# Moving the adapter products of the next two tiles, and the copies around them, in a two-adapter kernel

## The chip, the core and the metric

The kernel runs on one core of one Trainium2 chip. The metric is the device time of one execution in microseconds. Five engines work side by side: PE (TensorE, matmuls), DVE (VectorE), ACT (ScalarE), POOL (GpSimd) and SP (SyncE, which only issues transfers here). Each engine works through its own list of instructions in order, and an instruction that waits for a semaphore holds up everything behind it on its engine.

## What is computed

The input is 64 sequences of 64 rows with 1024 columns, so 4096 rows. First each sequence gets the correction of its own low-rank adapter (rank 16, picked by an index), then a dense layer with eight low-rank experts, of which the two best are weighed by a softmax. Both are added to their input.

```python
def _L0_cond_ref(x, A, B, adapter_ids):
    Bx = jnp.einsum('bni,bri->bnr', x, B[adapter_ids])
    return jnp.einsum('bnr,bor->bno', Bx, A[adapter_ids])        # SCALING is 1
def _L1_cond_ref(x, language_ids, W, Wr, A, B):
    base = jnp.einsum('btd,od->bto', x, W)
    logits = jnp.einsum('btd,ed->bte', x, Wr)                    # + 5.0 at the row's language
    topw, topi = jax.lax.top_k(logits, 2)
    gates = jnp.sum(jax.nn.one_hot(topi, E) * jax.nn.softmax(topw)[..., None], axis=-2)
    h = jnp.einsum('btd,erd->bter', x, A)
    return base + 2.0 * jnp.einsum('bter,bte,eor->bto', h, gates, B)
x = x + _L0_cond_ref(x, L0_cond_A, L0_cond_B, itok_B_4_50)
x = x + _L1_cond_ref(x, itok_B_0_7, L1_cond_W, L1_cond_Wr, L1_cond_A, L1_cond_B)
```

## The kernel before

The 4096 rows are 32 tiles of 128 rows. Every number is split into a high and a low part (`_hi`, `_lo`), and a product is made of three matmuls. The order of the work on each engine is written out by hand, and semaphores tie the engines together.

**What a tile needs.** DVE turns x (`turn_x_half`, `xT_part`), the rows of B (`bT_part`) and of A (`aT_part`). PE makes the B products (`make_bx`). ACT swaps halves of the result (`swap_part`), DVE adds them (`bx_half_part`), ACT shifts quarters (`pair_part`), and four DVE instructions (`bx_rest`) make `bx_t`. With it and the A rows PE makes the L0 products (`add_l0`), which add the first adapter into the bank that holds x. ACT and DVE split the sum into high and low parts, and PE multiplies it with the weights. The first 512 columns of that product hold the experts' rows and the router's logits. DVE chooses the experts (`choose_experts`) and weighs them (`weigh_experts`, whose last instruction makes `gated`; ACT makes one exponential, `exp_part`), PE turns `gated` (`turn_gated`), DVE copies it (`gated_t_part`, which makes `gt_hi` and `gt_lo`), and PE adds the expert products (`add_lora`, `pair_lora`; "lora products" below).

**Direct tiles.** Tiles 0 to 7 (`K = 8`) are multiplied in full, three parts each (`make_part`), in a loop over `n`. `bx_tiles(n)` says for which tiles the loop makes B products at the start of `n`: tile 2 at n=1, two tiles at n=2, 4 and 6, tile 9 at n=7. Meanwhile POOL makes sums of weight blocks (`t_chunk`, ten instructions each, four chunks, and `t_chunk_lo`, two each), which ACT rounds (`t_split`). In tile `n` DVE runs, in order: `bx_half` and `bx_rest` of the tiles in `bx_tiles(n)`, `choose_experts`, `weigh_experts`, `x1_lo_part(n+1)`, `gated_t_part(n)`, then transposes.

**Pairs.** Tiles 8 to 31 are twelve pairs `q` of tiles `a` and `b`. Each pair's other columns take seven products of block sums instead of eight. PE runs per pair: first columns of `a` (`pair_first_part(q, 0)`, 24 matmuls of 512 columns), four products of 12 matmuls each with `turn_gated(a)` among them, lora products of `a`, B products of `a+2`, first columns of `b`, L0 products of `a+2`, B products of `b+2`, two products, `turn_gated(b)`, one product, lora products of `b`, L0 products of `b+2`. In all pairs but the last the work for the next two tiles is woven in (`more`). `z_out` tells PE that ACT has copied the first columns out of their bank.

## Time and profile before

| | us |
|---|---|
| median of 3 runs (lowest, highest) | 548.58 (547.61, 553.17) |
| the profiled execution | 550.68 |
| its span, first to last instruction | 548.9 |
| mean granted TensorE clock | 0.988 |

| engine | busy us | share of the span |
|---|---|---|
| PE | 516.4 | 94% |
| DVE | 383.7 | 70% |
| POOL | 278.8 | 51% |
| ACT | 274.6 | 50% |

PE is busy nearly throughout, so the time is the sum of its products and of the short stretches in which it waits. Twelve pairs of nearly equal length follow the direct tiles, the first of them from 167.74 us. Where the page or an answer names a wait, the engine that was waited for stands behind the arrow. Such a row is read with the question what made that engine late.

### The profile page before, as it was taken

The page shows a single profiled execution, that of the slowest core. Times are in us where ns is not written, and L with a number is a line of the kernel's source. Part 1 is how long each engine was busy: PE and PEld are TensorE (multiplying, and loading weights), DVE is VectorE, ACT ScalarE, POOL GpSimd, SP SyncE. Part 2 cuts the span into 40 slices and gives each one's busy share as a digit, 9 for nine tenths or more (in the row PEclk, how much of TensorE's full clock was granted, in tenths as well). Part 3 has the DMA queues.
Part 4 walks back from the last instruction along what each step waited for, and adds up shares of the span by engine and source line. Part 5 has one row for each costly group of instructions (what it writes and reads, how often), then busy time and mean ns, then how long its engine had stood idle before and what let it go on. Part 6 is the DMA issues. An engine that isn't in the chain of part 4 may idle for free.

```text
span 548.9 us, 9809 instructions
## 1 busy us (share of the span) xinstructions
PE 516.4 (94%) x3356; PEld 462.6 (84%) x3356; DVE 383.7 (70%) x908; ACT 274.6 (50%) x617; POOL 278.8 (51%) x259
## 2 busy tenths in 40 slices
PE   7799999699989999999999999999998999999997
PEld 6688899599879878897987889898888989888896
DVE  5769666656857868586776858687685868777622
ACT  5446433333355645646464564555465554646521
POOL 5443328949975844455353545536354454535020
PEclk9699999999999999999999999999999999999999
DMA  8933523432242241524234151424316142430201
GB/s 311 325 95 100 144 77 95 125 92 87 73 125 87 83 169 39 168 70 128 97 102 149 39 189 60 133 81 111 141 53 193 43 135 78 114 136 1 79 27 51
DMA packets 31158, 60.45 MB, mean 110 GB/s; under 512 B 4348, under 2 KB 20476, under 8 KB 31108
## 3 DMA queue, kind: packets, MB, share of 16 engines
...
q8 instruction: 27, 0.44, 0.3%
...
## 4 chain that ended last, share of the span: by engine, by line
PE 63%; DVE 14%; issue 7%; ACT 6%; POOL 6%; DMA 4%; ACTq 0%; DVEq 0%; POOLq 0%
PE o_bank L730 24%; PE o_bank L739 12%; PE x_bank L739 9%; PE o_bank L706 5%; PE x_bank L612 4%; DMA a_in<-in_L_cond_A_dram,a_run 4%; ACT bx_pair L936 3%; PE b_bank L588 2%; PE o_bank L693 2%; DVE xs L1191 2%; PE x_bank L706 2%; POOL a_t L429 2%; POOL t_raw L493 2%; PE o_bank L682 2%; DVE bx_all L1342 1%
## 5 line engine op out<-in xcount | busy, mean ns | idle before, releaser
L730 PE MATMUL o_bank<-w_hi,xs 128*128 128x512 f32 x384 | 125.9, 399 | 0.1
L529 POOL TENSOR_TENSOR xs<-xt,xs 128x512 fp32r<-128x512 f32 x36 | 47.1, 1308 | 118.2 <-ACT xs L996 69.2
L693 PE MATMUL o_bank<-w_hi,xs 128*128 128x324 f32 (+1 forms) x336 | 91.8, 347 | 0.0
L730 PEld LDWEIGHTS o_bank<-w_hi,xs 128*128 128x128 f32 x384 | 72.1, 188 | 18.0 <-issue 2.2
L540 POOL TENSOR_TENSOR a_t<-a_raw,a_t 64x1024 fp32r<-64x1024 f32 x22 | 52.9, 2403 | 45.0 <-DVE bx_t L1349 44.0
L730 PE MATMUL o_bank<-w_lo,xs 128*128 128x512 f32 x192 | 75.4, 392 | 0.0
L400 POOL DMA_INDIRECT a_in<-in_L_cond_A_dram,a_run x64 | 60.8, 950 | 19.4 <-issue 19.2
L1314 DVE STREAM_TRANSPOSE a_raw<-a_in 128x1024 f32<-128x1024 f32 x32 | 64.7, 2021 | 2.8 <-DMA a_in<-in_L_cond_A_dram,a_run 2.8
L693 PEld LDWEIGHTS o_bank<-w_hi,xs 128*128 128x128 f32 x336 | 60.7, 191 | 5.5 <-issue 1.0
L1234 DVE STREAM_TRANSPOSE xt<-x_near 128x512 f32<-128x512 f32 x48 | 57.9, 1209 | 0.5 <-issue 0.5
L693 PE MATMUL o_bank<-w_lo,xs 128*128 128x324 f32 (+1 forms) x168 | 57.3, 341 | 0.0
L1191 DVE TENSOR_TENSOR xs<-x_bank,xs 128x512 fp32r<-128x512 f32 x64 | 43.2, 684 | 16.3 <-ACT xt L978 16.1
L1065 ACT ACTIVATE expd<-top 128x1 f32<-128x1 f32 x32 | 9.4, 295 | 82.6 <-DVE top L1369 82.6
L739 PE MATMUL x_bank<-t_w,xs 128*128 128x324 f32 x288 | 48.2, 315 | 0.0
L739 PE MATMUL o_bank<-w_hi,xs 128*128 128x324 f32 x192 | 47.9, 316 | 0.0
L739 PE MATMUL x_bank<-w_hi,xs 128*128 128x324 f32 x192 | 47.9, 316 | 0.0
L739 PEld LDWEIGHTS x_bank<-t_w,xs 128*128 128x128 f32 x288 | 43.6, 188 | 2.3 <-issue 2.2
L936 ACT COPY bx_pair<-bx_half 32x128 f32<-32x128 f32 x120 | 35.5, 296 | 19.0 <-DVE bx_half L1334 16.6
L730 PEld LDWEIGHTS o_bank<-w_lo,xs 128*128 128x128 f32 x192 | 36.2, 188 | 7.5
L909 ACT CAST a_t<-a_raw 128x1024 fp32r<-128x1024 f32 x32 | 33.6, 1051 | 17.1 <-DVE a_raw L1314 16.8
L406 POOL DMA_INDIRECT b_in<-in_L_cond_B_dram,b_run x32 | 30.8, 964 | 20.1 <-DVE a_t L1191 8.8
L1044 ACT COPY out_sb<-o_bank 128x376 f32<-128x376 f32 (+1 forms) x36 | 16.2, 460 | 44.9 <-PE o_bank L706 44.9
...
## 6 DMA issues: line engine op xcount, KB each, us to landing
...
a_in<-in_L_cond_A_dram,a_run POOLq DMA_INDIRECT x64, 3.5
...
```

Source lines behind the costliest of these rows:

```text
L400: pool.indirect_dma_start(a_in[:, m % 2, b, :], None, l0_A_runs, bass.IndirectOffsetOnAxis(ap=a_run[:, m * BPT + b:m * BPT + b + 1], axis= ...
L529: nc.gpsimd.tensor_tensor(xs[:, slot, 1, :, :], raw, xs[:, slot, 0, :, :].bitcast(F32), ALU.subtract).then_inc(ss_lo, 1)
L540: nc.gpsimd.tensor_tensor(lower, a_raw[Q:P, m % 2, :], lower.bitcast(F32), ALU.subtract)\
L693: mm = pe.matmul(O[part][:, 0:hi - lo], x1_at(n, c // CB, low)[:, c % CB, :], w[:, c, lo:hi], start=(k == 0), stop=(k == K3 - 1), skip_gro ...
L706: mm = pe.matmul(bank_out[:, skip:skip + hi - lo], gt[:, n % 2, :], lb[:, lo:hi], start=False, stop=(k == 2), skip_group_check=True)
L730: mm = pe.matmul(O[0][:, 0:hi - lo], xs[:, raw_slot(j, c // CB), low, c % CB, :], w[:, c, lo:hi], start=(k == 0), stop=(k == K3 - 1), skip ...
L739: mm = pe.matmul(bank_out[:, 0:H], xs[:, slot, low, c, :], w[:, c, :], start=(start and k == 0), stop=(k == 3 * CB - 1), skip_group_check= ...
L909: nc.scalar.copy(a_t[:, m % 2, :], a_raw[:, m % 2, :]).then_inc(a_hi_ready, 1)
L936: nc.scalar.copy(bx_pair[q * SQ:(q + 1) * SQ, :], bx_half[o * SQ:(o + 1) * SQ, :]).then_inc(pair_ready, 1)
L1191: return nc.vector.tensor_tensor(dst, raw, hi.bitcast(F32), ALU.subtract)
L1234: nc.vector.transpose(xt[:, m % 2, chunks(h), :].rearrange("p k (g i) -> p k g i", i=SQ), src[:, chunks(h), :, :]).then_inc(turned_s, 1)
L1314: nc.vector.transpose(raw.rearrange("p (k i f) -> p f k i", k=C, i=SQ), a_in[:, m % 2, :, :].rearrange("p b (f r) -> p f b r", r=R)).then_ ...
```

## The change

The B products of the next pair's both tiles now stand together, after 12 of the 24 matmuls of the first columns of `b` (`3 * CB` is 12). In the pairs ACT puts both halves of x into the bank ahead of the swaps, and copies x1 (`keep_raw`) ahead of `copy_cd`; DVE makes its transposes ahead of `bx_half(a+2)`, makes `aT_part(b+2)` between `bx_half(a+2)` and `bx_rest(a+2)`, and copies the turned gates of `b` ahead of `bx_rest(b+2)`. In the direct tiles `bx_rest` of the second of two tiles moves behind `weigh_experts`, and `turn_gated` waits accordingly for fewer steps. POOL's `t_chunk` run one tile earlier (m = 3 to 6 in place of 4 to 7), as does the place of ACT's `t_split` within its tile. The L0 products of tile 9 and the split of it move to the end of the direct tiles.

```diff
--- before.py
+++ after.py
@@ -514,15 +514,17 @@
                 pool.wait_ge(a_lo_ready, m + 1)
                 reload_b(m + 2)
                 reload_a(m + 2)
-                if 4 <= m < 4 + CB:
-                    if m == 4:
+                if m < 3 + CB:
+                    if m == 3:
                         pool.wait_ge(w_lo_dve, len(LO_DVE))
                         pool.wait_ge(w_lo_act, len(LO_ACT))
-                    t_chunk(m - 4)
-                    pool.wait_ge(t_step, 10 * (m - 3))
-                if m >= 6:
-                    t_chunk_lo(m - 6)
-                    pool.wait_ge(t_lo, 2 * (m - 5))
+                    t_chunk(m - 3)
+                    pool.wait_ge(t_step, 10 * (m - 2))
+                if m == 3 + CB:
+                    t_chunk_lo(0)
+                if m >= 3 + CB:
+                    t_chunk_lo(m - 2 - CB)
+                    pool.wait_ge(t_lo, 2 * (m - 1 - CB))
 
             def s_lo(q, which, slot, raw):
                 pool.wait_ge(ss_hi, 4 * q + which)
@@ -713,7 +715,7 @@
             def pair_lora(n, part, bank_out):
                 lora_products(n, part, bank_out).then_inc(so_psum, 1)
 
-            def pair_first_part(q, side):
+            def pair_first_part(q, side, bx=()):
 
                 j = 2 * q + side
                 if q == 0 and side == 0:
@@ -724,6 +726,9 @@
                 lo, hi = PARTS[0]
                 for k in range(K3):
                     c = k // 3
+                    if k == 3 * CB:
+                        for m in bx:
+                            make_bx(m)
                     if k % (3 * CB) == 0:
                         pe.wait_ge(sl_ready, HB * j + c // CB + 1)
                     low, w = ((0, w_hi), (0, w_lo), (1, w_hi))[k % 3]
@@ -821,15 +826,14 @@
                 make_part(n, 0, 0, K3).then_inc(h_psum, 1)
                 add_l0(n + 1)
                 make_part(n, 1, 0, K3)
-                turn_gated(n, bx_count(bx_made(n)))
+                turn_gated(n, bx_count(bx_made(n) - 1) + 1)
                 make_part(n, 2, 0, 12)
-                if n == K - 1:
-                    add_l0(K + 1)
                 pe.wait_ge(gt_ready, 2 * (n + 1))
                 add_lora(n, 0)
                 add_lora(n, 1)
                 make_part(n, 2, 12, K3)
                 add_lora(n, 2)
+            add_l0(K + 1)
 
             for q in range(PAIRS):
                 a, b = K + 2 * q, K + 2 * q + 1
@@ -856,12 +860,9 @@
                 pe.wait_ge(gt_ready, 2 * (a + 1))
                 pair_lora(a, 0, O[0])
                 pair_lora(a, 1, PA)
-                if more:
-                    make_bx(a + 2)
-                pair_first_part(q, 1)
+                pair_first_part(q, 1, (a + 2, b + 2) if more else ())
                 if more:
                     add_l0(a + 2)
-                    make_bx(b + 2)
                 pe.wait_ge(bc_copied, q + 1)
                 wait_sum(q, S1)
                 if q == 0:
@@ -1125,6 +1126,8 @@
                 exp_part(n)
                 if n + 1 < K:
                     x1_hi_part(n + 1)
+                if 3 <= n < 3 + CB:
+                    t_split(n - 3)
                 for m in turned(n)[1:] if n == 1 else turned(n):
                     xt_part(m)
                 if n == K - 2:
@@ -1136,17 +1139,12 @@
                 out_part(n, 1)
                 if n < K - 1:
                     a_hi_part(n + 2)
-                if n == K - 1:
-                    split_b(K + 1)
-                if 3 <= n < 3 + CB:
-                    t_split(n - 3)
                 out_part(n, 2)
 
             for q in range(PAIRS):
                 a, b = K + 2 * q, K + 2 * q + 1
                 more = b + 2 < T
-                if q > 0:
-                    split_b(b)
+                split_b(b)
                 s3_hi(q)
                 s2_hi(q)
                 if q == 0:
@@ -1166,20 +1164,19 @@
                 pair_out(a, 0, O[0], LA0, z_out)
                 pair_out(a, 1, PA, LA1, c11_out)
                 if more:
-                    swap_part(a + 2, a + 3)
-                    put_half(a + 2, 0)
+                    put_part(a + 2)
+                    swap_part(a + 2, b + 3)
                     pair_part(a + 2)
                     a_hi_part(b + 2)
-                    put_half(a + 2, 1)
                 exp_part(b)
                 if more:
                     raw_hi(a + 2, 0)
                     keep_raw(a + 2, 0)
                     swap_part(b + 2, b + 3)
                     raw_hi(a + 2, 1)
+                    keep_raw(a + 2, 1)
                 copy_cd(q)
                 if more:
-                    keep_raw(a + 2, 1)
                     pair_part(b + 2)
                     put_part(b + 2)
                 pair_out(b, 0, O[0], LB0, z_out)
@@ -1508,7 +1505,8 @@
             aT_part(2)
 
             for n in range(1, K):
-                for m in bx_tiles(n):
+                ahead = bx_tiles(n)[:1] if n % 2 == 0 else bx_tiles(n)
+                for m in ahead:
                     bx_half_part(m)
                     if n == 1:
                         xT_half(3, 0)
@@ -1516,10 +1514,12 @@
                 if n == 1:
                     a_lo_part(2)
                     xT_half(3, 1)
-                if n == K - 1:
-                    aT_part(K + 1)
+                for m in bx_tiles(n)[len(ahead):]:
+                    bx_half_part(m)
                 choose_experts(n)
                 weigh_experts(n)
+                for m in bx_tiles(n)[len(ahead):]:
+                    bx_rest(m)
                 if n + 1 < K:
                     x1_lo_part(n + 1)
                 else:
@@ -1534,33 +1534,34 @@
                     bT_part(m)
                 if n < K - 1:
                     aT_part(n + 2)
-                if n == K - 1:
-                    sums_of_pair(0)
+                if n == K - 2:
+                    aT_part(K + 1)
 
             for q in range(PAIRS):
                 a, b = K + 2 * q, K + 2 * q + 1
                 more = b + 2 < T
+                sums_of_pair(q)
                 if q == 0:
                     for c in range(CB):
                         t4_lo(c)
-                else:
-                    sums_of_pair(q)
-                if more:
+                if more and q > 0:
                     aT_part(a + 2)
                 choose_experts(a)
                 weigh_experts(a)
+                if q == 0:
+                    aT_part(a + 2)
                 if more:
                     turn_x_half(a + 2, 0)
                     bT_part(a + 2)
                 gated_t_part(a)
                 if more:
                     turn_x_half(a + 2, 1)
-                    aT_part(b + 2)
-                    bx_half_part(a + 2)
                     turn_x_half(b + 2, 0)
-                    bx_rest(a + 2)
                     turn_x_half(b + 2, 1)
                     bT_part(b + 2)
+                    bx_half_part(a + 2)
+                    aT_part(b + 2)
+                    bx_rest(a + 2)
                 choose_experts(b)
                 if more:
                     raw_lo(a + 2, 0)
@@ -1568,8 +1569,9 @@
                 if more:
                     raw_lo(a + 2, 1)
                     bx_half_part(b + 2)
+                gated_t_part(b)
+                if more:
                     bx_rest(b + 2)
-                gated_t_part(b)
                 out_b1(q)
                 out_b2(q)
```

On PE, around the first columns of tile `b` of a pair (here the first; `xt,b_raw` are B products, `bx_t,a_t` L0 products, `w_hi,xs` 128x512 the first columns), before:

```order
L706 MATMUL o_bank<-lb_hi,gt_lo 128x324
L588 MATMUL b_bank<-xt,b_raw 32x128 x8
L730 MATMUL o_bank<-w_hi,xs 128x512
...
L730 MATMUL o_bank<-w_hi,xs 128x512
L612 MATMUL x_bank<-bx_t,a_t 128x128 x8
L588 MATMUL b_bank<-xt,b_raw 32x128 x8
L739 MATMUL x_bank<-t_w,xs 128x324 x12
```

And of the change:

```order
L708 MATMUL o_bank<-lb_hi,gt_lo 128x324
L735 MATMUL o_bank<-w_hi,xs 128x512
...
L735 MATMUL o_bank<-w_hi,xs 128x512
L590 MATMUL b_bank<-xt,b_raw 32x128 x16
L735 MATMUL o_bank<-w_hi,xs 128x512
...
L735 MATMUL o_bank<-w_hi,xs 128x512
L614 MATMUL x_bank<-bx_t,a_t 128x128 x8
L744 MATMUL x_bank<-t_w,xs 128x324 x12
```

The B products no longer stand between the lora products and the first columns, nor behind the L0 products; both batches are inside the first columns, 12 matmuls ahead of the L0 products.

On DVE, the same stretch of a pair, from the copies of the turned gates of `a` to the choice of experts of `b`, before:

```order
L1191 TENSOR_TENSOR gt_lo<-b_bank,gt_hi 128x128
L1234 STREAM_TRANSPOSE xt<-x_near 128x512
L1314 STREAM_TRANSPOSE a_raw<-a_in 128x4x256
L1334 TENSOR_TENSOR bx_half<-b_bank,bx_swap 128x128
L1234 STREAM_TRANSPOSE xt<-x_near 128x512
L1342 TENSOR_TENSOR bx_all<-bx_half,bx_pair 128x128
L1344 TENSOR_TENSOR bx_own<-bx_all,own 128x128
L1346 CAST bx_hi<-bx_own 128x128
L1349 SCALAR_TENSOR_TENSOR bx_t<-bx_hi,minus_odd,bx_own 128x128
L1234 STREAM_TRANSPOSE xt<-x_near 128x512
L1306 STREAM_TRANSPOSE b_raw<-b_in 128x256
L1366 SCALAR_TENSOR_TENSOR logit<-is_lang,o_bank 128x8
```

And of the change:

```order
L1188 TENSOR_TENSOR gt_lo<-b_bank,gt_hi 128x128
L1231 STREAM_TRANSPOSE xt<-x_near 128x512 x3
L1303 STREAM_TRANSPOSE b_raw<-b_in 128x256
L1331 TENSOR_TENSOR bx_half<-b_bank,bx_swap 128x128
L1311 STREAM_TRANSPOSE a_raw<-a_in 128x4x256
L1339 TENSOR_TENSOR bx_all<-bx_half,bx_pair 128x128
L1341 TENSOR_TENSOR bx_own<-bx_all,own 128x128
L1343 CAST bx_hi<-bx_own 128x128
L1346 SCALAR_TENSOR_TENSOR bx_t<-bx_hi,minus_odd,bx_own 128x128
L1363 SCALAR_TENSOR_TENSOR logit<-is_lang,o_bank 128x8
```

All three transposes of x and the one of B stand ahead of `bx_half`, and the long transpose of A stands between `bx_half` and `bx_all`.

On DVE in the direct tiles (here n=2), from `bx_half` of the second tile on, before:

```order
L1334 TENSOR_TENSOR bx_half<-b_bank,bx_swap 128x128
L1342 TENSOR_TENSOR bx_all<-bx_half,bx_pair 128x128
L1344 TENSOR_TENSOR bx_own<-bx_all,own 128x128
L1346 CAST bx_hi<-bx_own 128x128
L1349 SCALAR_TENSOR_TENSOR bx_t<-bx_hi,minus_odd,bx_own 128x128
L1366 SCALAR_TENSOR_TENSOR logit<-is_lang,o_bank 128x8
```

And of the change:

```order
L1331 TENSOR_TENSOR bx_half<-b_bank,bx_swap 128x128
L1363 SCALAR_TENSOR_TENSOR logit<-is_lang,o_bank 128x8
...
L1390 TENSOR_TENSOR gated<-o_bank,gate 128x128
L1339 TENSOR_TENSOR bx_all<-bx_half,bx_pair 128x128
L1341 TENSOR_TENSOR bx_own<-bx_all,own 128x128
L1343 CAST bx_hi<-bx_own 128x128
L1346 SCALAR_TENSOR_TENSOR bx_t<-bx_hi,minus_odd,bx_own 128x128
L1188 TENSOR_TENSOR xs<-x_bank,xs 128x512 x2
L1396 CAST gt_hi<-b_bank 128x128
```

The four instructions of `bx_rest` leave the place ahead of the choice of experts and stand between `gated` and the copies of the turned gates.

## Rows read from the trace of the kernel before

**Rows 1.** Waits of PE over the whole span: waited for, us in total, times, longest.

```profile
PE o_bank L706 <- DVE gt_lo L1191: 10.5, 11, 1.1
PE b_bank L573 <- DVE gated L1393: 6.4, 3, 4.4
```

**Rows 2.** Timeline of PE, tiles 2, 4, 6, 7: start, us, operation, idle before.

```profile
68.22 1.00 PE L612 MATMUL x_bank<-bx_t,a_t 128*128 128x128 f32 x8
...
72.70 0.28 PE L573 MATMUL b_bank<-ident,gated 128*128 128x128 f32 x1
...
74.61 0.33 PE L706 MATMUL o_bank<-lb_hi,gt_hi 128*128 128x376 f32 x1
...
100.29 1.11 PE L612 MATMUL x_bank<-bx_t,a_t 128*128 128x128 f32 x8 [0.43 <-DVE bx_t L1349]
...
109.50 0.47 PE L573 MATMUL b_bank<-ident,gated 128*128 128x128 f32 x1 [4.44 <-DVE gated L1393]
...
112.78 0.33 PE L706 MATMUL o_bank<-lb_hi,gt_hi 128*128 128x376 f32 x1
...
143.79 0.33 PE L573 MATMUL b_bank<-ident,gated 128*128 128x128 f32 x1 [1.23 <-DVE gated L1393]
...
163.56 1.08 PE L612 MATMUL x_bank<-bx_t,a_t 128*128 128x128 f32 x8 [0.78 <-POOL a_t L429]
```

**Rows 3.** Stretches: us, busy PE, PEld, DVE, ACT, POOL, granted clock, DMA.

```profile
109.50:113.00 3.50, 3.50 (x15) 3.50 (x16) 3.46 (x6) 0.59 (x1) 1.30 (x2) 0.58 0.00 0
...
143.70:147.00 3.30, 3.21 (x21) 3.21 (x22) 3.27 (x7) 0.48 (x2) 3.06 (x5) 1.00 0.00 0
```

**Rows 4.** Timeline of POOL, tiles 2 and 3.

```profile
68.97 0.95 POOL L400 DMA_INDIRECT a_in<-in_L_cond_A_dram,a_run  x1 [0.30 <-issue]
80.13 2.39 POOL L429 TENSOR_TENSOR a_t<-a_raw,a_t 64x1024 fp32r<-64x1024 f32 x1 [10.21 <-ACT a_t L909]
```

**Rows 5.** Timeline of DVE in tile 4.

```profile
101.83 0.97 DVE L1342 TENSOR_TENSOR bx_all<-bx_half,bx_pair 128x128 f32<-128x128 f32 x1 [1.39 <-ACT bx_pair L936]
...
109.16 0.29 DVE L1393 TENSOR_TENSOR gated<-o_bank,gate 128x128 f32<-128x128 f32 x1
...
110.87 0.29 DVE L1191 TENSOR_TENSOR gt_lo<-b_bank,gt_hi 128x128 fp32r<-128x128 f32 x1
```

**Rows 6.** Timeline of PE, a pair in the middle, from its lora products of `a`.

```profile
339.68 0.34 PE L706 MATMUL o_bank<-lb_hi,gt_hi 128*128 128x376 f32 x1
...
346.99 1.00 PE L612 MATMUL x_bank<-bx_t,a_t 128*128 128x128 f32 x8
347.92 0.64 PE L588 MATMUL b_bank<-xt,b_raw 128*32 128x128 f32 x16
...
352.66 0.30 PE L573 MATMUL b_bank<-ident,gated 128*128 128x128 f32 x1 [0.29 <-DVE bx_half L1334]
...
355.75 0.44 PE L706 MATMUL o_bank<-lb_hi,gt_hi 128*128 128x376 f32 x1 [0.92 <-DVE gt_lo L1191]
...
358.55 0.45 PE L730 MATMUL o_bank<-w_hi,xs 128*128 128x512 f32 x1
```

**Rows 7.** Chain that ended last, same pair: start, us, work.

```profile
341.38 5.77 PE o_bank L730 x24
```

**Rows 8.** Timelines of ACT and of DVE, same pair.

```profile
341.44 0.55 ACT L929 COPY bx_swap<-b_bank 64x128 f32<-64x128 f32 x2 [0.17 <-PE b_bank L588]
...
331.45 2.01 DVE L1314 STREAM_TRANSPOSE a_raw<-a_in 128x1024 f32<-128x1024 f32 x1
333.31 0.16 DVE L1366 SCALAR_TENSOR_TENSOR logit<-is_lang,o_bank 128x8 f32<-128x8 f32 x1
...
342.02 0.29 DVE L1334 TENSOR_TENSOR bx_half<-b_bank,bx_swap 128x128 f32<-128x128 f32 x1 [0.27 <-ACT bx_swap L929]
...
343.86 0.29 DVE L1342 TENSOR_TENSOR bx_all<-bx_half,bx_pair 128x128 f32<-128x128 f32 x1 [0.43 <-ACT bx_pair L936]
...
344.77 0.35 DVE L1349 SCALAR_TENSOR_TENSOR bx_t<-bx_hi,minus_odd,bx_own 128x128 fp32r<-128x128 f32 x1
```

**Rows 9.** Timeline of PE, last pair, lora products of `a` and first columns of `b`.

```profile
530.42 0.34 PE L706 MATMUL o_bank<-lb_hi,gt_hi 128*128 128x376 f32 x1
...
531.67 0.50 PE L730 MATMUL o_bank<-w_hi,xs 128*128 128x512 f32 x1
```

## Prediction

> **What bounds the kernel now.** I read the waits of PE first, then its timeline through the direct tiles and through one pair in the middle, and only then the engines that it waits for. PE is busy 94% of the span, and the change leaves out none of its products, so it can only win or lose waits and the slow products that follow them. The waits that repeat are these. In the pairs PE waits 11 times, once in each pair that has a next one, for the copies of the turned gates of `b` [rows 1]: 0.92 us at 355.75, and 0.29 us at 352.66 for `bx_half` of the tile after next [rows 6]. In the direct tiles it waits three times for `gated`, 6.4 us together, of which 4.44 us in tile 4 [rows 1, 2], and 0.78 us for POOL ahead of the L0 products of tile 9 [rows 2]. A whole pair takes about 31.8 us, of which these waits are 1.2 us, so no edit of the waits can give much more than 4% of a pair.
>
> **The direct tiles.** A tile without a wait is the scale: from its L0 products to the turn of its gates 4.48 us (68.22 to 72.70), from there to its lora products 1.91 us, 6.39 us together [rows 2]. Tile 4 took 12.49 us from 100.29, and 0.43 us of waiting ahead of that, so it lost 6.5 us. Not all of this is waiting: after 4.44 us without work the granted clock was 0.58 in the stretch that follows [rows 3], near the lower level of 1.2 GHz, and the turn stood 3.28 us ahead of the lora products in place of 1.91. The cause is on DVE. `bx_rest` of tile 6 stands ahead of the choice of experts and meets `t_chunk(1)` on POOL; `bx_all` took 0.97 us there [rows 5] and 0.29 us in a pair, where POOL is quiet [rows 8].
>
> The change puts `bx_rest` of the second tile behind `gated`. So `gated` of tile 4 comes some 2.2 us after the L0 products (my estimate for twelve small instructions, 2.7 where POOL slows the last), against 4.48 needed, and this wait goes. What is late next is the copy of the turned gates: behind `gated` stand now the four instructions of `bx_rest` and the two of `x1_lo_part`. From the start of `gated` to the end of `gt_lo` without `bx_rest` were 2.0 us (109.16 to 111.16 [rows 5]). With `bx_rest` under POOL, 3.4 to 3.9 us (four of up to 0.97), PE's lora products find them after 2.2 + 2.0 + 3.7 = 7.9 us, where they come after 6.39. That is a new wait of 1.5 us in tile 4, and 1.2 in tile 6, where POOL has only four instructions of `t_chunk_lo`. In tile 2 nothing was lost, but `t_chunk(0)` now starts right behind the transfers issued at 68.97 (its ten instructions end near 79.5, ahead of POOL's next work at 80.13, so they delay nothing on POOL) [rows 4], and meets both the weighing and `bx_rest`: 2.7 + 2.0 + 3.7 - 6.39 = 2.0, of which I take 1.9. From below these new waits are zero: with `bx_rest` at the 1.3 us that it takes beside a quiet POOL (343.86 to 345.12 [rows 8]) the copies are ready after 5.5 us.
>
> Here a rule of the Trainium skill can be weighed. SBUF — State Buffer, section Who interferes with whom, says that DVE and GpSimd share a pair of ports as an exclusive lock, and that a DVE instruction with two SBUF inputs or in a two-port mode waits until the other's instruction is done. By that rule the price of 3.7 us holds wherever `bx_rest` meets POOL's products; the trace agrees in tile 4 (0.97 against 0.29). By the cheap rows the sum below would be 4.6 us lower.
>
> Then the rest of the direct tiles. The other two waits for `gated`, 6.4 - 4.4 = 2.0 us, go, because `bx_rest` or `aT_part(9)` no longer stand ahead of the choice. The 0.8 us for POOL's part of tile 9 goes, because these L0 products move behind all lora products of tile 7, 3 us later, and DVE's transpose for it comes a tile earlier. Restarts after these waits cost about 0.2 us each, 0.4 together. POOL's `t_chunk` and ACT's `t_split` one tile earlier cost nothing themselves: they run beside PE, and no copy on ACT now waits for POOL ahead of a swap. Sum: +1.9 (tile 2) - 6.5 + 1.5 (tile 4) + 1.2 (tile 6) - 2.0 - 0.8 - 0.4 = -5.1 us.
>
> **A pair.** I walk one pair with the rows' own times.
> 1. The first columns of `b` follow the lora products of `a` directly, and their bank must first be copied out. The last pair has no B products there and shows the price: 530.42 to 531.67, 1.25 us [rows 9]. So they start at 339.68 + 1.25 = 340.93 [rows 6] (six lora products alone take about 0.96, so 0.3 is a new wait that the B products covered).
> 2. The 24 products take 5.7 us [rows 7], and the two batches of B products between them about 1.2 (0.64 each, overlapping [rows 6]). PE reaches the L0 products at 347.8.
> 3. The chain to `bx_t`: 12 products, 343.8; B products, 345.05; the swap, then 0.58 to `bx_half` (341.44 to 342.02), 345.65; then DVE does `aT_part(b+2)`, which takes 1.86 us before the next instruction begins (331.45 to 333.31), 347.75. The four copies of `pair_part` lie beside it. `bx_rest` takes 1.26, so `bx_t` is there at 349.0 [rows 8]. POOL is idle then, and the port costs nothing. New wait: 1.2 us. The L0 products begin at 349.0, against 346.99: +2.0.
> 4. The turn of `b`'s gates comes without the B batch (-0.6) and without the 0.29 wait: +1.1. `bx_half(b+2)` must be ready for it: I get 353.55 against PE's arrival at 353.75, because x1 is kept ahead of `copy_cd` on ACT. That is a thin cover.
> 5. The lora products follow after 1.9 us, as in tile 2 [rows 2], in place of 3.09 (352.66 to 355.75 [rows 6]), since only the turn stands ahead of the copies: -0.1.
> 6. From there 2.80 us to the next pair (358.55), of which 0.1 is a slow restart after the wait: -0.2.
>
> The x and B transposes of `b+2` end near 342.7, a microsecond ahead of the B products at 343.8; were that cover gone, the wait would come in step 2 and not add to that of step 3 in full. POOL's part of A for `b+2` and its transfers start some 4 us later than now and still end ahead of the next pair's use by about as much. So a pair wins 0.2 us, 11 pairs 2.2. By the bounds: if `aT_part` did not count, step 3 would be bound by the pair copies and the wait 0.7 (11 pairs: -7); if step 4 or 5 each lose 0.3, a pair loses 0.4 (+4.5). I take the value between, as every step of it has a row.
>
> **The first pair.** Its transpose of A for tile 10 moves behind the weighing, and ACT's conversion of it stands ahead of the copies that release the first columns of `b`. It can cost between nothing and the transpose's 2.01 us [rows 8]; I take 0.9.
>
> **Sum.** -5.1 + 0.9 - 2.2 = -6.4 us. The profiled execution took 550.68 us (548.9 inside its span), so it would be 544.3; it stands 2.1 above the median of 548.58, from which the same sum gives **542.2 us**.
>
> **Rivals.**
> - *The pairs give the gain back.* Step 4's thin cover fails, or `bx_t` comes later than 349.0: 0.3 us lost per pair is +3.3 in place of -2.2. Time 548.6 - 5.1 + 0.9 + 3.3 = 547.7. For it: the new waits, 0.3 + 1.2, are as long as the old ones, 0.92 + 0.29. Against it: two slow restarts become one. 0.26.
> - *The direct tiles give little.* Moving `bx_rest` behind `gated` only hands the wait on, and waits of 2 to 3 us in tiles 2, 4 and 6 bring slow products too: -2 in place of -5.1, time 545.3. Against it: the tile 6 wait of 1.23 us left the granted clock at 1.00 [rows 2, 3]. 0.12.
> - *The transpose hides.* With the wait of step 3 at 0.7, time 537.4. For it: the pair copies end before the transpose by only 0.5 us. Against it: the order on DVE is fixed, the transpose stands ahead. 0.08.
> - *Slower: the clock falls in every pair.* If the new wait of 1.2 us ahead of the L0 products lowered the granted clock as 4.44 us did in tile 4, where the turn to lora stretch grew by 1.4 us (3.28 - 1.91 [rows 2, 3]), 11 pairs would cost 15 us and the time be 557. It decides from a loss of 1.1 us per pair. Against it: the wait of 1.23 us in tile 6 was followed by a stretch at a granted clock of 1.00 [rows 2, 3]. 0.05.
> - The forecast itself: 0.49.
>
> **The numbers.** The likeliest time is 542.2, and by itself it would lie between 540 and 545. The range of 537 to 548 takes in the bounds of the pairs and the first two rivals; it leaves out the slower one and the far ends. About 1%, 5.5 us, is what a measurement of this kernel can tell from no change; 543.1 is that border, not far from the forecast. Faster by over 1%: most of the forecast (0.40 of 0.49), the hidden transpose 0.08 and a little of the second rival 0.04, so 0.52. Same is 0.42, and slower 0.06, the falling clock and a loss in the pairs beyond the bounds of step 3.
>
> **What would show it.** Right: in the waits of PE, the row for `gt_lo` in pairs and the one for `bx_half` are gone or nearly, and there are 11 waits of about 1.2 us of the L0 products for `bx_t`; pairs 31.6 us apart; no wait of 4 us in tile 4, but waits of the lora products for `gt_lo` of 1 to 2 us in tiles 2, 4 and 6; the first columns of tile 8 near 162.6 in place of 167.7. Wrong: a wait at `turn_gated(b)` for `bx_half` of more than 0.3 us, a wait of the B products inside the first columns, a granted clock below 1 in the pairs, or `bx_rest` near 1.3 us in tile 2 in spite of `t_chunk(0)`.

## The result, and the profile after

The changed kernel took 558.11 us in the median (557.70 to 560.40), the kernel before beside it 550.33 (547.61 to 553.17): a ratio of 1.0149 [1.0083, 1.0216]. The forecast was 542.2. The change made the kernel slower by 1.5%, where the forecast had it faster, and the time lies outside the forecast range of 537 to 548 us.

Waits of PE in the trace after, as waited for, us in total, times, longest (span 555.9 us, granted clock 0.988 in the mean):

```profile
PE x_bank L614 <- DVE bx_t L1346: 11.5, 11, 1.1
PE b_bank L575 <- DVE bx_half L1331: 8.4, 11, 0.8
PE o_bank L708 <- DVE gt_lo L1188: 7.7, 4, 3.1
```

The 11 waits for `gt_lo` in the pairs [rows 1] are gone. The 11 for `bx_t` are there, as forecast, and so are 11 for `bx_half` of 0.77 us, for which the forecast had none. One pair on PE:

```profile
343.30 0.34 PE L708 MATMUL o_bank<-lb_hi,gt_hi 128*128 128x376 f32 x1
347.56 1.08 PE L590 MATMUL b_bank<-xt,b_raw 128*32 128x128 f32 x32
352.64 1.11 PE L614 MATMUL x_bank<-bx_t,a_t 128*128 128x128 f32 x8 [1.05 <-DVE bx_t L1346]
358.17 0.30 PE L575 MATMUL b_bank<-ident,gated 128*128 128x128 f32 x1 [0.77 <-DVE bx_half L1331]
360.17 0.33 PE L708 MATMUL o_bank<-lb_hi,gt_hi 128*128 128x376 f32 x1
```

This answers to [rows 6]. To compare kernels I use the turn of the gates of tile `a` (L575 here, L573 before), whose place in a pair the change leaves alone. Before, it came at 178.64 in the first pair, 210.65 in the second and 528.52 in the last, so the ten pairs between took 31.79 us each. After, it came at 177.89, 211.76 and 535.80: 32.40 each. So the 7.0 us by which the span grew are -0.75 up to the first pair (the direct tiles), +1.86 in the first pair, +6.17 in the next ten, and -0.28 behind that. Of the -0.75, 0.22 lie ahead of tile 0's turn, where the two kernels do the same work, so the direct tiles themselves gave 0.53.

DVE and POOL around the new wait:

```profile
352.24 0.35 DVE L1346 SCALAR_TENSOR_TENSOR bx_t<-bx_hi,minus_odd,bx_own 128x128 fp32r<-128x128 f32 x1
...
352.97 0.16 DVE L1368 FIND_INDEX8 top_at<-top,logit 128x8 uint32<-128x8 f32 x1
353.17 2.03 DVE L1370 CAST top_no<-top_at 128x2 f32<-128x2 uint32 x1
355.11 0.68 DVE L1188 TENSOR_TENSOR xs<-x_bank,xs 128x512 fp32r<-128x512 f32 x1
...
356.94 0.29 DVE L1390 TENSOR_TENSOR gated<-o_bank,gate 128x128 f32<-128x128 f32 x1
...
357.75 0.28 DVE L1331 TENSOR_TENSOR bx_half<-b_bank,bx_swap 128x128 f32<-128x128 f32 x1
```

```profile
352.79 2.38 POOL L542 TENSOR_TENSOR a_t<-a_raw,a_t 64x1024 fp32r<-64x1024 f32 x1 [8.17 <-DVE bx_t L1346]
355.44 0.96 POOL L406 DMA_INDIRECT b_in<-in_L_cond_B_dram,b_run  x1 [0.27 <-POOL a_t L542]
```

A cast of two columns takes 2.03 us and ends with POOL's product. In the trace before it took 0.17 us in the tiles `b` (0.32 in the first pair); after, 2.03 us in all 11 that have a next pair. This suggested the first theory.

### The profile page after: what moved, and what is told of

Read it like the earlier page. It is cut to its first block, busy times and chain, and to the rows that moved or that the text cites. A ratio compares the mean times of both kernels' runs of the same rounds, so it can differ in the third digit from the quotient of the medians.

```text
span 555.9 us, 9808 instructions
## 1 busy us (share of the span) xinstructions
PE 515.4 (93%) x3356; PEld 460.7 (83%) x3356; DVE 402.7 (72%) x908; ACT 275.3 (50%) x617; POOL 279.3 (50%) x259
## 4 chain that ended last, share of the span: by engine, by line
PE 66%; DVE 21%; issue 6%; ACT 4%; DMA 1%; POOL 1%; ACTq 0%; DVEq 0%; POOLq 0%
PE o_bank L735 18%; PE o_bank L695 12%; PE o_bank L744 11%; PE x_bank L744 8%; PE o_bank L708 5%; DVE a_raw L1311 4%; DVE xs L1188 4%; PE x_bank L614 3%; DVE top_no L1370 3%; PE b_bank L590 3%; PE o_bank L684 2%; PE x_bank L708 2%; DMA a_in<-in_L_cond_A_dram,a_run 1%; DVE bx_all L1339 1%; DVE bx_own L1341 1%
## 5 line engine op out<-in xcount | busy, mean ns | idle before, releaser
L735 PE MATMUL o_bank<-w_hi,xs 128*128 128x512 f32 x384 | 128.7, 401 | 2.2 <-ACT out_sb L1045 0.9
L1231 DVE STREAM_TRANSPOSE xt<-x_near 128x512 f32<-128x512 f32 x48 | 54.8, 1192 | 0.3 <-issue 0.3
L614 PEld LDWEIGHTS x_bank<-bx_t,a_t 128*128 128x128 f32 x256 | 32.9, 195 | 16.8 <-DVE bx_t L1346 16.2
L614 PE MATMUL x_bank<-bx_t,a_t 128*128 128x128 f32 x256 | 34.1, 277 | 11.5 <-DVE bx_t L1346 11.5
```

Source lines behind the costliest of these rows:

```text
L614: mm = pe.matmul(bx_bank(m, h)[:, c * P:(c + 1) * P], a_t[:, m % 2, d:d + P], bx_t[:, m % 2, :], start=False, stop=True, skip_group_check= ...
L735: mm = pe.matmul(O[0][:, 0:hi - lo], xs[:, raw_slot(j, c // CB), low, c % CB, :], w[:, c, lo:hi], start=(k == 0), stop=(k == K3 - 1), skip ...
L1231: nc.vector.transpose(xt[:, m % 2, chunks(h), :].rearrange("p k (g i) -> p k g i", i=SQ), src[:, chunks(h), :, :]).then_inc(turned_s, 1)
```

## Two theories, and what could tell them apart

*Collision*: POOL's part of A, let go by `bx_t` and so moved from beside DVE's transposes to beside the choice of experts, stretches the cast, and that makes the wait for `bx_half`. *Order*: `bx_half(b+2)` is the last of a line on DVE (`raw_lo` of half 0, weighing, `raw_lo` of half 1), the first of which waits for ACT's copies behind the L0 products; this line is too long even without a collision. The two can also add up. A third point is the split of the loss between pairs and direct tiles.

One thing stood in the way. Beside the experiments the kernel before itself took 573.6, 553.0, 581.3, 573.1 and 573.8 us in the five comparisons (the first four of them hold four kernels each), where it took 550.3 beside the change. The section on `d17_before_itself` shows why: ACT or DVE stand still there for some microseconds with nothing that visibly holds them. Such a pause is called a stop below. So totals are compared with the kernel before only where that took 553 us or less. Elsewhere I read single waits, and two stretches that each trace shows: from the start to the turn of `a` in the first pair (called *start*), and from there to the end (*pairs*). The turn of tile 0 comes between 38.8 and 41.5 us in all these traces, and up to it all kernels do the same, so the second column of the table takes it off. The stretches are those of the profiled execution, which can lie some microseconds beside the median (c13: 557.96 against 562.78).

| kernel | start, us | start behind tile 0's turn, us | pairs, us | median, us |
| --- | --- | --- | --- | --- |
| before | 178.6 | 137.3 | 370.2 | 550.3 |
| after | 177.9 | 136.7 | 378.0 | 558.1 |
| a5_after_again | 179.9 | 140.4 | 378.2 | 559.4 |
| a6_pool_again | 178.4 | 138.2 | 375.1 | 555.5 |
| a7_pool_weigh | 179.6 | 138.2 | 382.2 | 562.6 |
| a8_pool_weigh_turn | 178.2 | 136.8 | 378.5 | 558.1 |
| b10_pairs_mended | 181.7 | 141.1 | 362.2 | 544.3 |
| b12_both | 181.0 | 140.3 | 364.5 | 545.4 |
| c14_mended_again | 178.6 | 137.2 | 362.5 | 542.9 |
| c15_mended_chunk | 174.8 | 134.4 | 362.3 | 539.6 |
| d18_mended_chunk_again | 175.2 | 134.7 | 362.4 | 540.2 |
| x3_before_collide | 178.5 | 137.2 | 370.4 | 551.4 |
| c13_pairs_only_third | 176.2 | 137.4 | 379.9 | 562.8 |
| c16_direct_only_again | 180.2 | 140.5 | 393.6 | 574.5 |
| d17_before_itself | 181.0 | 140.1 | 390.0 | 572.8 |

## Experiments on the pairs

**a5_after_again.** No edit.

> The changed kernel, nothing edited. Its trace had pairs of 32.41 us, 11 waits of 1.05 us for bx_t and 11 of 0.77 us for bx_half, and the cast of top_no at 2.03 us for tile b of each pair. If these belong to the program, they come back to within 0.05 us, and the ratio to the kernel before is 1.01 to 1.02. If the loss belonged to the chip of the first comparison, the ratio is elsewhere while the waits are the same.

559.42 us beside 553.02: 1.0114 [1.0080, 1.0148]. Pairs of 32.39 us, waits of 11.4 and 8.4 us in total, the cast 2.03 us in 11 tiles. The loss and its waits belong to the program.

**x1_pool_after_choice and a6_pool_again.** One wait more on POOL, ahead of the second `a_lo_paired`:

```diff
                     pool.wait_ge(bx_step, bx_count(a + 3))
+                    pool.wait_ge(gate_step, GATE * (a + 1) + 4)
                     a_lo_paired(a + 3, a + 3, a + 3)
```

> The changed kernel, with POOL's part of A (a_t) made to wait for the cast of top_no of tile b, as in x1_pool_after_choice. Theory collision (POOL's instruction locks out the cast of top_no, 2.03 us, and that makes the wait of the turn for bx_half): top_no 0.17 us, that wait 0 us, pairs 31.65 us, total 8 us below the changed kernel. Theory order (raw_lo of half 0, which waits for ACT's copies behind L0, stands ahead of the weighing, and that sets bx_half; the collision adds little): the wait of the turn for bx_half stays at 0.5 us, pairs 32.1 us, total 3 us below the changed kernel.

The first of the two ran beside the kernel before at 573.6 us and gave 566.57 (I had expected 549 to 550 by collision, above 554 without), with stops of ACT of up to 3.7 us. The second, the same program, gave 555.50 beside 553.02: 1.0049 [1.0022, 1.0076]. Its waits of PE:

```profile
PE x_bank L615 <- DVE bx_t L1347: 11.4, 11, 1.1
PE o_bank L709 <- DVE gt_lo L1189: 7.0, 4, 3.1
PE b_bank L576 <- DVE bx_half L1332: 5.3, 11, 0.5
```

The cast is back at 0.17 us, pairs are 32.11 us, and the wait for `bx_half` is 0.49 us in place of 0.77. That is the number that theory order had named. But the collision is not gone from this kernel. Its DVE and its POOL:

```profile
352.25 0.17 DVE L1371 CAST top_no<-top_at 128x2 f32<-128x2 uint32 x1
353.60 0.69 DVE L1189 TENSOR_TENSOR xs<-x_bank,xs 128x512 fp32r<-128x512 f32 x1 [1.18 <-ACT xt L980]
...
354.59 0.47 DVE L1382 TENSOR_TENSOR weight<-weight,expd 128x1 f32<-128x1 f32 x1
...
355.96 0.68 DVE L1189 TENSOR_TENSOR xs<-x_bank,xs 128x512 fp32r<-128x512 f32 x1
356.55 0.28 DVE L1332 TENSOR_TENSOR bx_half<-b_bank,bx_swap 128x128 f32<-128x128 f32 x1
```

```profile
352.64 2.40 POOL L542 TENSOR_TENSOR a_t<-a_raw,a_t 64x1024 fp32r<-64x1024 f32 x1 [8.89 <-DVE top_no L1371]
```

POOL now starts behind the cast, and its 2.40 us end at 355.04. The product for the second weight starts at 354.59, takes 0.47 us in place of 0.16, and ends when POOL does, in all 11 pairs. Nothing behind it waits for ACT (its second copy is done at 355.17, and `raw_lo` starts at 355.96), so these 0.31 us are in the line too. Without any collision `bx_half` would let the turn go 4.94 us behind the start of the L0 products (my estimate: 5.25 less 0.31), against 5.53 in the change, and the wait would be 0.18 us.

The trace after gives the same by itself: ACT's first copy was done at 354.41, `raw_lo` starts 0.10 us behind that copy in a6, and in the change it started at 355.11, so 0.60 us late. The collision is thus worth 0.6 us a pair, about as much as the pair lost (0.62). Theory order explains the smaller rest of the wait. No run holds POOL behind `gated` and changes nothing else, so this split stands on rows and not on a run of its own.

The order is a fact all the same: after the cast DVE stands for 1.18 us for ACT's copy, and the weighing, whose inputs have long been there, stands behind that.

**a7_pool_weigh.** As a6, and the weighing goes ahead:

```diff
                 choose_experts(b)
-                if more:
-                    raw_lo(a + 2, 0)
                 weigh_experts(b)
                 if more:
+                    raw_lo(a + 2, 0)
                     raw_lo(a + 2, 1)
```

> As a6_pool_again, and DVE weighs the experts of b before it makes the low part of the first half of the next x1 (raw_lo(a+2, 0) behind weigh_experts(b)). Theory order: the weighing no longer waits for ACT's copies behind L0, gated and bx_half come about 1.1 us sooner, the wait of the turn for bx_half is gone, pairs 31.6 us, total 5 to 6 us below a6_pool_again. Theory collision: no wait was left, so pairs and total as a6_pool_again.

A miss for both theories: 562.55 us, 1.0178 [1.0133, 1.0222], pairs of 32.73 us, and the wait for `bx_half` grew to 1.1 us. Its DVE and its POOL:

```profile
356.65 0.17 DVE L1371 CAST top_no<-top_at 128x2 f32<-128x2 uint32 x1
356.73 0.15 DVE L1378 TENSOR_SCALAR half_sum<-expd 128x1 f32<-128x1 f32 x1
356.91 0.17 DVE L1380 RECIPROCAL weight<-half_sum 128x1 f32<-128x1 f32 x1
357.11 2.35 DVE L1382 TENSOR_TENSOR weight<-weight,expd 128x1 f32<-128x1 f32 x1
...
360.14 0.29 DVE L1391 TENSOR_TENSOR gated<-o_bank,gate 128x128 f32<-128x128 f32 x1
```

```profile
357.04 2.40 POOL L542 TENSOR_TENSOR a_t<-a_raw,a_t 64x1024 fp32r<-64x1024 f32 x1 [8.91 <-DVE half_sum L1378]
```

The weighing now follows at once and meets POOL: a product of one column takes 2.35 us. The wait on POOL was one step too short already in a6, where POOL's instruction was nearly over when the product came; here it has just begun.

The instructions that wait for POOL are the cast, the products and sums with both inputs in SBUF and the scalar products of eight columns (the scalar product of one column, the reciprocal and the transposes are no longer beside POOL than alone); `gated`, `raw_lo` and `bx_half`, which read one operand from a PSUM bank, keep their 0.29, 0.68 and 0.28 us. The Trainium skill says it so (SBUF — State Buffer, section Who interferes with whom): a DVE instruction with two SBUF inputs, or a cast or scalar product in a two-port mode, contends with GpSimd, and whoever issues first has the shared ports for its whole instruction. These traces agree, and put the price at POOL's rest (2.03 us for the cast, 2.35 for the product, 0.47 in a6), whatever the size of DVE's own work.

**a8_pool_weigh_turn.** As a7, and the transpose of A goes ahead:

```diff
+                    aT_part(b + 2)
                     bx_half_part(a + 2)
-                    aT_part(b + 2)
                     bx_rest(a + 2)
```

> As a7_pool_weigh, and the 2.0 us transpose of A for b+2 on DVE stands ahead of bx_half(a+2) instead of behind it, in the 2.6 to 3.1 us in which DVE waits for the swap. The wait of the L0 products for bx_t falls from 1.05 us to about 0.6 us, what the four copies of pair_part leave; pairs 31.15 us, total 5 us below a7_pool_weigh and 5 to 8 us below the kernel before. If instead the transpose's data are not there yet at that point, bx_half comes later and the wait grows above 1.05 us.

558.11 us, 4.4 below a7, ratio 1.0099 [1.0063, 1.0135]. The wait for `bx_t` fell to 0.7 us (7.7 in total), pairs are 32.40 us: 0.33 less than in a7, of the 0.45 expected. The other two figures missed, pairs of 31.15 us and a time below the kernel before, because the wait for `bx_half` stayed at 1.1 us as in a7.

**b10_pairs_mended and c14_mended_again.** The direct tiles of before, the pair edits of the change, the two edits of a7 and a8, and POOL held back until `gated` of `b` is made:

```diff
                     pool.wait_ge(bx_step, bx_count(a + 3))
+                    pool.wait_ge(gate_step, GATE * (a + 2))
                     a_lo_paired(a + 3, a + 3, a + 3)
```

> As b9_pairs_only_again, with three edits of the pair: POOL's part of A for b+2 waits until gated of b is made (so that its 2.4 us meet neither the choice nor the weighing), DVE weighs the experts of b ahead of raw_lo(a+2, 0), and its transpose of A for b+2 stands ahead of bx_half(a+2). Theory order and lock together: in a7 the lock only moved, from the cast of top_no (2.03 us) to the product for the second weight (2.35 us); with POOL behind gated no small instruction of DVE is stretched, gated is there about 2.5 us after L0 begins, the wait of the turn for bx_half is gone, the wait for bx_t is 0.65 us; pairs 31.2 us, total 1.2 us times 11 = 13 us below b9_pairs_only_again. If something else sets bx_half (ACT's swap of b+2, or its copies), that wait stays above 0.3 us and the pairs at 31.6 or more.

544.26 us; pairs of 31.09 us. Its rows of PE, DVE and POOL:

```profile
347.91 1.11 PE L613 MATMUL x_bank<-bx_t,a_t 128*128 128x128 f32 x8 [0.70 <-DVE bx_t L1349]
352.49 0.30 PE L574 MATMUL b_bank<-ident,gated 128*128 128x128 f32 x1
```

```profile
348.89 0.16 DVE L1384 TENSOR_TENSOR weight<-weight,expd 128x1 f32<-128x1 f32 x1
...
349.68 0.29 DVE L1393 TENSOR_TENSOR gated<-o_bank,gate 128x128 f32<-128x128 f32 x1
349.89 0.68 DVE L1191 TENSOR_TENSOR xs<-x_bank,xs 128x512 fp32r<-128x512 f32 x1
351.46 0.69 DVE L1191 TENSOR_TENSOR xs<-x_bank,xs 128x512 fp32r<-128x512 f32 x1 [0.88 <-ACT xt L979]
352.06 0.28 DVE L1334 TENSOR_TENSOR bx_half<-b_bank,bx_swap 128x128 f32<-128x128 f32 x1
```

```profile
350.19 2.40 POOL L540 TENSOR_TENSOR a_t<-a_raw,a_t 64x1024 fp32r<-64x1024 f32 x1 [9.50 <-DVE gated L1393]
```

The turn follows the L0 products after 4.58 us, in place of 5.53 in the change, and waits for nothing; POOL's 2.40 us lie beside instructions with a PSUM operand. What DVE waits for now is ACT's second copy, 0.88 us, and that fits. The three edits act together here; a7 and a8 had two of them with POOL still in the way.

> As b10_pairs_mended (pair edits of the change, with POOL's part of A behind gated of b, the weighing ahead of raw_lo, the transpose of A ahead of bx_half). Pairs of 31.08 us as there against 31.79: 7 us over ten pairs, ratio to an undisturbed kernel before 0.985 to 0.990. If the gain of b10 was only a matter of where the stops fell, the ratio is 0.995 or more.

542.88 us in the median of three executions (a fourth took 706.57), pairs of 31.09 us. The ratios beside these two (0.9356 and 0.9497) say little, since the kernel before was at 581 and 573 us. The stretch *pairs* says it better: 362.2 to 362.5 us in four traces of three comparisons, 7.9 below the undisturbed kernel before and 15.6 below the change. A fifth trace with the same pair edits, b12, has 364.5, of which 1.5 are a single wait of PE for ACT in one pair.

**x3_before_collide.** The kernel before, with POOL's part of A moved beside the choice:

```diff
                     pool.wait_ge(bx_step, bx_count(a + 3))
+                    pool.wait_ge(gate_step, GATE * (a + 1) + 3)
                     a_lo_paired(a + 3, a + 3, a + 3)
```

> The kernel before with one added wait on POOL: its part of A for tile b+2 starts after the third instruction of the choice of experts of b, so beside the cast top_no. Nothing else is changed. Theory P: top_no takes 2 us or more in each pair, and the pair grows by about 1 us or more, 11 times: 558 to 563. Rival A: the cast stays at 0.17 us or its length costs nothing, time within 2 us of the kernel before.

It missed the cast, since POOL's part of A starts only behind it: no cast over 0.37 us. But it met the next instruction, as in a6:

```profile
350.03 0.53 DVE L1385 TENSOR_TENSOR weight<-weight,expd 128x1 f32<-128x1 f32 x1
```

That is 0.53 us in place of 0.16, and from the second pair on it costs nothing: pairs of 31.77 us, and the wait for `bx_half` is 3.5 us in total where it was 3.2, the 0.3 all in the first pair. In the order of before, `raw_lo` of half 1 waits 0.61 us for ACT's copy behind this point, and takes the 0.37 us up. So a collision counts only where the line behind it has no such wait, and in the change it has none. The run took 551.40 us beside the kernel before at 573.57, from one wait on POOL that changes no time of PE from the second pair on against the undisturbed trace before.

## Experiments on the split, and on the direct tiles

**x2_pairs_only, b9_pairs_only_again, c13_pairs_only_third.** The kernel before with the pair hunks of the diff alone, one program run three times.

> The pair edits of the change alone (as b9_pairs_only_again), on another chip. Open is how the loss of 5 to 8 us splits between pairs and direct tiles, since in the two comparisons of this kernel so far the kernel before itself took 573 and 581 us, and ACT and DVE stood still in places where nothing held them. Where they don't: pairs of 32.4 us, ratio 1.009 to 1.014, so that the pairs are the loss. With the stops in: pairs 32.7 to 32.9, and a ratio that says nothing of the change.

563.87, 568.61 and 562.78 us, beside kernels before at 573.6, 581.3 and 573.1: the stops were in each time, so the totals stay useless. What can be read is the waits (c13):

```profile
PE x_bank L612 <- DVE bx_t L1348: 12.0, 12, 1.1
PE b_bank L573 <- issue: 7.8, 10, 0.8
```

and that the cast took 2.03 us in 11 tiles in each of the three. The pair edits alone bring both waits of the change and the stretch *pairs* of 379.9 us, against 378.0 with the direct edits too. So nothing that the direct tiles hand on is needed to explain the loss in the pairs. The 379.9 itself holds stops (pairs of 32.70 us where the change has 32.40). The first pair is another matter: it takes 32.70 us with the pair edits alone (c13 and x2) and 33.87 in the change, so 1.2 us of its loss come from the direct edits and the passage.

**x4_direct_only, c16_direct_only_again.** The direct tiles of the change with the pairs of before.

> The direct tiles of the change alone, with the pairs of before. In the traces of the changed kernel the second pair began 1.3 and 3.2 us later than in the kernel before, whatever the pairs did. If the direct tiles gave the 5.1 us of the forecast, ratio 0.99; if they only hand the wait on, with slow products behind it in tile 2 and in some executions in tile 4, 1.000 to 1.007, and the executions spread over 3 us or more.

572.15 and 574.49 us, beside 573.57 and 573.11: 0.9973 and 0.9982 [0.9933, 1.0031]. Both are disturbed. The stretch *start* is 180.2 us in c16, and over all traces 177.9 to 180.2 with the change's direct tiles and 176.2 to 181.7 with those of before. Taken from tile 0's turn, it is 136.7 to 138.2 or 140.4 to 140.5 with the change's, and 137.2 to 137.4 or 140.1 to 141.1 with those of before. So the change gives the direct tiles 0.5 us at best, and nothing that these runs can show for sure.

The spread with the change's tiles has a source that can be read. The wait in tile 4 for `gt_lo` was 3.0 to 3.2 us in each trace of the change's direct tiles. After it, the granted clock in the trace after (first fence, from 109 and 113 us) and in a5 (second) was:

```profile
109.00:113.00 4.00, 1.55 (x11) 1.28 (x9) 3.92 (x6) 0.00 (x0) 3.84 (x5) 1.00 0.00 0
113.00:117.00 4.00, 3.38 (x22) 3.30 (x22) 3.97 (x7) 1.77 (x4) 1.28 (x2) 1.00 0.00 0
117.00:121.00 4.00, 4.00 (x19) 3.27 (x19) 1.18 (x1) 1.49 (x3) 1.60 (x1) 1.00 0.12 48
```

```profile
109.00:113.00 4.00, 1.05 (x7) 0.77 (x6) 3.89 (x8) 0.00 (x0) 3.77 (x6) 0.91 0.00 0
113.00:117.00 4.00, 3.92 (x14) 3.92 (x15) 4.00 (x5) 1.88 (x4) 0.81 (x1) 0.50 0.00 0
117.00:121.00 4.00, 4.00 (x18) 3.65 (x17) 0.53 (x1) 1.48 (x2) 2.26 (x1) 0.73 0.09 38
```

The same program and the same wait: once the clock stayed at its upper level, once it fell to the lower (0.50, 1.2 GHz) for about 7 us in these three stretches, and tile 5's turn came 21.1 us behind tile 4's in place of 18.5. The same wait of 3 us cost 2.6 us more in one execution than in the other.

**b11_chunk_later.** The kernel before, with the collision of tile 4 taken away at POOL:

```diff
+                    if m in (5,):
+                        pool.wait_ge(gt_ready, 2 * m)
                     t_chunk(m - 4)
```

> The kernel before with one wait more on POOL: t_chunk(1) begins only when the copies of the turned gates of tile 4 are made. Theory lock: DVE's bx_rest(6), choice and weighing of tile 4 then take what they take beside a quiet POOL, the wait of 4.44 us of the turn for gated in tile 4 falls to under 0.5 us, the clock stays at its upper level behind it, and the time falls by 5 to 6.5 us (ratio 0.989), with no wait of POOL handed on, since it stood idle for 6 us behind t_chunk(1). If the order on DVE and not the lock set the wait, it stays above 2 us.

582.90 us beside 581.30: 1.0013 [0.9972, 1.0054]. The cause was right: `bx_rest(6)` takes 0.29 us an instruction, and tile 4's turn comes at 104.36 with a wait of 0.21 us, where it came at 109.50 after 4.44 [rows 2]. But tile 5's comes at 125.33, only 0.65 us earlier than before, and no earlier when the turn of tile 0 (40.52 against 41.37) is taken off. PE and POOL between them:

```profile
104.36 0.33 PE L575 MATMUL b_bank<-ident,gated 128*128 128x128 f32 x1 [0.21 <-DVE gated L1395]
...
117.81 1.94 PE L614 MATMUL x_bank<-bx_t,a_t 128*128 128x128 f32 x8 [2.54 <-issue]
...
125.33 0.27 PE L575 MATMUL b_bank<-ident,gated 128*128 128x128 f32 x1
```

```profile
106.10 0.88 POOL L493 TENSOR_TENSOR t_raw<-w_hi 128x324 f32<-128x324 f32 x1 [5.31 <-DVE gt_lo L1193]
...
115.37 2.34 POOL L429 TENSOR_TENSOR a_t<-a_raw,a_t 64x1024 fp32r<-64x1024 f32 x1
```

POOL is late with its part of A for tile 6 (done at 117.7), PE waits 2.54 us ahead of its L0 products (`<-issue`: the profile names nothing that released it, but they start 0.1 us behind POOL), and from there to the turn it needs 7.5 us in place of 4.5, at a granted clock of 0.56 from 117 to 121 us. I had counted POOL's idle 6 us without seeing that PE, 5 us earlier, would ask for the result 5 us earlier too.

**b12_both.** b10 with this wait in tile 4 and one like it for `t_chunk(3)` in tile 6.

> b10_pairs_mended and b11_chunk_later together, and t_chunk(3) held back likewise behind the gates of tile 6 (where the wait for gated is 1.23 us). If the parts add up: 6.5 us of the pairs, 5 to 6 us of tile 4 and 1 us of tile 6 below the kernel before, ratio 0.975 to 0.985. If the late t_chunk(3) makes POOL late for the first pair, a wait for a_t or t_w of 1 us or more shows there and the ratio is near 0.985.

545.38 us, no better than b10. The second bound came true and more: from tile 6's turn to tile 7's it took 21.7 us in place of 16.9, with a wait of 3.6 us ahead of L0 products.

**c15_mended_chunk and d18_mended_chunk_again.** b10, and in tile 4 POOL held only until `gated`, 1.8 us less:

```diff
+                    if m == 5:
+                        pool.wait_ge(gate_step, GATE * m)
                     t_chunk(m - 4)
```

> As c14_mended_again, and t_chunk(1) on POOL held back until gated of tile 4 is made. In b11 it was held until the copies of the turned gates, 1.7 us later, and so POOL's part of A for tile 6 was 2.54 us late, which gave the won 5 us back (slow clock behind it included). Here that wait is 0.8 us by the same rows, and the clock stays up: the turn of tile 4 has no wait, tile 5's comes at 120.5 to 121.5, and the total is 3 to 5 us below c14_mended_again. If the wait for a_t is 2 us or more again, or the clock falls, the total is as c14_mended_again.

539.56 us (538.89 to 540.25), 3.3 below c14 beside it. Of the stretches, *start* behind tile 0's turn shows 2.8 of them. PE in tiles 4 to 6:

```profile
104.26 0.33 PE L576 MATMUL b_bank<-ident,gated 128*128 128x128 f32 x1 [0.22 <-DVE gated L1395]
...
116.05 1.08 PE L615 MATMUL x_bank<-bx_t,a_t 128*128 128x128 f32 x8 [0.93 <-issue]
...
140.38 0.33 PE L576 MATMUL b_bank<-ident,gated 128*128 128x128 f32 x1 [1.37 <-DVE gated L1395]
```

The wait for POOL is 0.93 us, the granted clock 1.00 behind it, and tile 5's turn comes at 120.61, 5.4 us ahead of the kernel before (4.4 with tile 0's turn taken off). In tile 6 2.0 of these are lost again: its wait for `gated` is 1.37 us, and `bx_t` of its first products came 1.73 us late.

> As c15_mended_chunk, to measure it against the kernel before on another chip: 537 to 541 us. Beside a kernel before of 549 to 553 us the ratio is 0.975 to 0.985; beside one of 570 to 580 us it is 0.935 to 0.95.

540.15 us (539.03 to 541.09) beside 573.82: 0.9429 [0.9393, 0.9465]. That ratio holds on chips on which the kernel before is disturbed. Against its undisturbed 550.33 and 553.02 us of other comparisons, 540 is 1.9 to 2.3% less; no interval can be given for that.

**d17_before_itself.** No edit.

> The kernel before itself, profiled beside the others. Its times were 548 to 554 us in two of the comparisons and 570 to 585 us in three. If it is again above 565 us, its trace shows ACT or DVE standing still for 1 to 4 us in every pair with nothing released, and pairs of 33 us or more in place of 31.8; the difference between comparisons is then in these stops, and not in a wait that the change touches. If it is near 550 us, the trace has no such stops, and the ratio of the next kernel is one to an undisturbed kernel before.

572.76 us. The ten pairs took 33.76 us each in place of 31.79. In one of them:

```profile
325.97 2.07 PE L739 MATMUL x_bank<-t_w,xs 128*128 128x324 f32 x12
```

```profile
329.62 0.41 ACT L1031 COPY o_bank<-x_bank 128x324 f32<-128x324 f32 x1 [1.72 <-remote]
```

This copy needs the 12 products above, done by 328.04. In the first trace it began 0.03 us behind them, here 1.6 us, and no row of any engine or transfer ends at that moment (`<-remote`: no instruction of this core is named as what released it). DVE then stands 2.15 us ahead of `raw_lo`, where it stood 0.61, and the turn waits 1.8. Six of the eleven pairs have this stop. Other kernels have it elsewhere, always in the same place of a pair: 3.3 us of DVE at L1283 in all three runs of the pairs-only kernel, up to 3.7 us of ACT at L1046 in x1, where a6, the same program on another chip, had none. The large ones stood behind a product of PE. In the ten pairs of this trace the turn waits 16 us more than in the trace before. Behind four of these waits, of 1.83 to 1.89 us, the granted clock fell to 0.50 (0.95 in the mean of the pair, pairs of 34.1 us), behind two others of 1.86 and 1.87 us it stayed at 1.00 (pairs of 33.3). Together that explains nearly all of the 19.7 us. What causes the stops is open. The transfers of instructions lie within 2 us of this one, but over 200 us of this trace they did not go along with the stops.

## Why the prediction was wrong

- **Step 1** (first columns 1.25 us behind the lora products) and **step 3** (`bx_t` sets the L0 products) held. The L0 products came 9.34 us behind the lora products of `a`, forecast 9.32; the wait is 1.05, forecast 1.2.
- **Step 4 failed.** PE reached the turn 4.76 us behind the start of the L0 products, as forecast, but `bx_half(b+2)` let it go only 5.53 us behind it; the forecast had it ready after 4.55. PE waited 0.77 us a pair, 8.4 us over 11, and that is nearly all of the 0.8 us by which a pair missed its forecast. Two terms failed.
  - The collision was put at nothing: "POOL is idle then, and the port costs nothing". That was right for `bx_rest` and wrong behind it, since it is `bx_t` itself that lets POOL go, and the choice of experts follows it at once. It costs 0.6 us a pair (0.28 measured between the change and a6, 0.31 estimated from a6's rows). What stood on record ahead of the result has both facts, the late part of A on POOL and the choice right behind `bx_t`, and does not put them in one row.
  - The gain of x1 kept ahead of `copy_cd` was mis-sized. The forecast lets `bx_half` come 1.1 us sooner behind the L0 products than the 5.67 of [rows 6]; without the collision it would be 0.7 (5.67 less 4.94, by the estimate above). In the trace before, `raw_lo` of half 1 had waited only 0.61 us for that copy, and then DVE's own line is the bound:

```profile
351.63 0.69 DVE L1191 TENSOR_TENSOR xs<-x_bank,xs 128x512 fp32r<-128x512 f32 x1 [0.61 <-ACT xt L978]
```

- **Steps 5 and 6** held: the lora products followed after 2.00 us (forecast 1.9), and from there to the next pair it was 2.69 us in place of 2.80, the 0.1 that was forecast. Together a pair lost 0.62 where it was to win 0.2, nearly all of it by step 4.
- **The direct tiles** gave 0.75 us in place of 5.1, of which 0.2 lie ahead of tile 0's turn. From turn to turn: tile 2 to 3 took 4.5 us more (forecast +1.9; the wait was 2.71, and slower products behind it cost 1.6, at a granted clock of 0.74 from 76 to 80 us); tile 3 to 4 5.3 less and tile 4 to 5 2.1 more (together -3.2, forecast -5.0); tile 6 to 7 0.7 more (forecast +1.2); the others 2.5 less (forecast -3.2 with the restarts). `bx_rest` under `t_chunk` did take 0.84 to 0.98 us an instruction, as said, and from `gated` to the end of `gt_lo` it was 5.6 us (forecast 5.7). The term that was mis-sized is the one ahead of it, `gated` behind the L0 products. It was put at 2.7 us in tile 2 and 2.2 in tile 4 and came after 3.56 and 3.93, since POOL's `t_chunk` met two instructions of the weighing in tile 2 and three in tile 4, and not the last one alone. So the waits were 2.7 and 3.1 us in place of 1.9 and 1.5. The second term is the slow products behind such waits, which the forecast left to a rival.
- **The first pair** lost 1.86 us; the forecast was 0.7 with its share of the pair gain. Of the excess of 1.2 us 0.8 is that of every pair; the 0.9 put on the passage itself measured 1.2.
- **The rivals.** "The pairs give the gain back" named the failing step, and "the direct tiles give little" the other one. Each was priced alone, at 547.7 and 545.3; both came true, and the first at twice its price. The slower rival, a clock that falls in each pair, did not happen: the granted clock was 1.00 from 178 to 536 us. That its time of 557 us lies near the measured one is chance. In "the transpose hides", 11 times 0.7 is 7.7 and not 7, which would have made it 536.7.

The signs written down were the right ones: a wait of over 0.3 us at `turn_gated(b)` was named as what would prove the forecast wrong.
